# Expert rounds of a two-layer kernel: the next pair's first product ahead of the convolution, and ScalarE's weight copies behind it

## What is computed

```
xn = layernorm(x)
u, v = xn @ Wu + bu, xn @ Wv + bv
y = (u * causal_fft_conv(v, h)) @ Wo + bo
per token: top-2 of 8 experts by softmax(xn @ Wg)
   expert e: relu(xn @ W1[e] + b1[e]) @ W2[e] + b2[e]   (128 -> 256 -> 128)
x = x + y + sum over the two experts of probability * expert output
```

## Time and profile before

| | us |
|---|---|
| median of three runs | 493.45 (492.63 to 493.6) |
| the profiled execution, its own time | 493.04 |
| its span, first to last instruction | 491.2 |
| PE matmul busy | 366.0 (75%), weight loads 298.7 (61%) |
| DVE busy | 294.4 (60%) |
| ACT busy | 225.9 (46%) |
| POOL busy | 258.4 (53%) |

### The profile page before, as it was taken

The page is one execution under the profiler, slowest core; times in us unless marked ns, Lnnn a source line. Parts: engine busy times, 40 slices in busy tenths (PEclk is TensorE's granted clock), DMA queues, the critical chain, the costliest instruction groups (busy, mean ns, idle before and its releaser), DMA issues.

```text
span 491.2 us, 7805 instructions
## 1 busy us (share of the span) xinstructions
PE 366.0 (75%) x2302; PEld 298.7 (61%) x2302; DVE 294.4 (60%) x782; ACT 225.9 (46%) x551; POOL 258.4 (53%) x254
## 2 busy tenths in 40 slices
PE   2485588869997975949997978898887777766720
PEld 0272255658675644737996867787776667755620
DVE  3977569614773796474688993478438772244105
ACT  1373042325332316334343066434567676687724
POOL 2754766733666323016566676666666555365540
PEclk9999599997998999687998999999999999999975
DMA  9999999823321330001111282445322215422407
GB/s 211 396 197 262 166 140 135 268 51 85 87 75 40 111 89 1 1 5 39 34 34 37 69 261 75 142 140 151 112 69 75 63 29 158 137 74 74 126 11 252
DMA packets 64744, 55.05 MB, mean 112 GB/s; under 512 B 6819, under 2 KB 56683, under 8 KB 64446
## 3 DMA queue, kind: packets, MB, share of 16 engines
q1 hardware_dynamic: 57888, 41.71, 35.6%
q0 software_dynamic: 6656, 12.51, 8.4%
q10 hardware_dynamic: 158, 0.33, 0.4%
HBM read 30.44 MB, written 25.27 MB: 113 GB/s over the span
## 4 chain that ended last, share of the span: by engine, by line
PE 44%; issue 13%; ACT 12%; DVE 10%; DMA 10%; POOL 8%; SPq 1%; ACTq 0%; POOLq 0%; DVEq 0%
PE psS L1161 19%; PE psO L1161 15%; PE psT L1161 7%; ACT hT L1122 7%; POOL slots L826 4%; DMA slots<-row,slot 4%; DMA moe<-ys,xs 2%; POOL w L847 2%; DMA xres<-in_x 2%; ACT row L1027 1%; PE psT L1263 1%; POOL moe L836 1%; DVE work L1713 1%; DVE xres L1747 1%; DMA moe<-ys,ring 1%
## 5 line engine op out<-in xcount | busy, mean ns | idle before, releaser
L813 POOL DMA_INDIRECT slots<-row,slot x64 | 69.3, 1083 | 57.0 <-DVE slot L1580 22.4
L836 POOL DMA_INDIRECT moe<-ys,xs x61 | 61.1, 1001 | 58.3 <-issue 16.6
L1161 PE MATMUL psO<-ring,hT 128*128 128x128 f32 x320 | 45.2, 284 | 45.1 <-ACT hT L1122 45.1
L1161 PEld LDWEIGHTS psO<-ring,hT 128*128 128x128 f32 x320 | 38.7, 191 | 53.4 <-issue 53.4
L1122 ACT ACTIVATE hT<-psT,ring 128x128 f32<-128x128 f32 x160 | 45.6, 368 | 45.7 <-PE psT L1161 45.7
L1868 DVE TENSOR_TENSOR ys<-psO,ring 128x256 f32<-128x256 f32 x40 | 17.0, 424 | 75.3 <-PE psO L1161 75.1
L1055 ACT ACTIVATE ring<-w 128x642 f32 x80 | 55.9, 761 | 1.1 <-issue 1.0
L1161 PE MATMUL psS<-work 128*128 128x512 f32 (+3 forms) x96 | 42.6, 558 | 12.6 <-DVE work L1696 8.8
L836 POOL DMA_INDIRECT moe<-ys,w x35 | 38.0, 1087 | 23.3 <-DVE ys L1868 9.7
L1020 ACT ACTIVATE work<-psT 128x512 f32<-128x512 f32 (+3 forms) x32 | 16.5, 516 | 66.6 <-PE psT L1263 66.6
L826 POOL DMA_INDIRECT slots<-row,slot x32 | 34.9, 1091 | 18.1 <-DMA slots<-row,slot 10.9
(11 more groups left out here) (272 smaller groups left out, 781.4 us busy)
## 6 DMA issues: line engine op xcount, KB each, us to landing
slots<-xs SPq DMA_DIRECT2D x14, 516.0 KB, 14.7
mats<-in_iv SPq DMA_DIRECT2D x16, 256.0 KB, 3.7
xs<-slots SPq DMA_DIRECT2D x61, 64.5 KB, 1.9
w<-in_w SPq DMA_DIRECT2D x8, 321.0 KB
w<-slots SPq DMA_DIRECT2D x35, 64.5 KB, 1.9
xres<-in_x SPq DMA_DIRECT2D x4, 512.0 KB, 9.7
mats<-in_fw SPq DMA_DIRECT2D x1, 2048.0 KB, 11.3
moe<-xs SPq DMA_DIRECT2D x4, 512.0 KB, 7.8
```

What stands on the lines that cost most here:

```text
L813: pool.indirect_dma_start(slots1[:, :], bass.IndirectOffsetOnAxis(ap=(slot1, slot2)[k][:, i:i + 1], axis=0), row[:, i, :], None, bounds_ch ...
L836: pool.indirect_dma_start(dst[:, :], bass.IndirectOffsetOnAxis(ap=row_slots[l][m][:, D:ROWW].bitcast(I32), axis=0), ys[:, n % UNROLL, :], ...
L1161: return pe.matmul(o, lhsT, rhs, start=start, stop=stop)
```

## The change

On TensorE `expert_hidden(r + 1)` moves up, directly behind `expert_out(r)` and ahead of the convolution. On ScalarE `hidden(r + 1)` moves to the front of the round, and `copy_weights(r + 2)` from the front to behind the convolution's copies, directly ahead of `take_rows(r + 2)`. No instruction is added or removed; VectorE, GpSimd and SyncE keep their order.

```diff
             for r in range(PRELUDE, PAIRS1):
-                if 0 <= r + 2 < PAIRS1:
-                    copy_weights(r + 2)
+                if 0 <= r + 1 < PAIRS1:
+                    hidden(r + 1)
                 for kind, k in conv_at(r):
...
                     if kind == "yt":
                         take_y(k)
-                if 0 <= r + 1 < PAIRS1:
-                    hidden(r + 1)
                 if 0 <= r + 2 < PAIRS1:
+                    copy_weights(r + 2)
                     take_rows(r + 2)
...
             for r in range(PRELUDE, PAIRS1):
                 if 0 <= r:
                     expert_out(r)
+                if 0 <= r + 1 < PAIRS1:
+                    expert_hidden(r + 1)
                 for kind, k in conv_at(r):
...
                     if kind == "wo":
                         project_y(k)
-                if 0 <= r + 1 < PAIRS1:
-                    expert_hidden(r + 1)
                 if 0 <= r + 2 < PAIRS1:
                     expert_rows(r + 2)
```

## The result

| | before | after |
|---|---|---|
| median, us | 493.04 (491.58 to 493.6, 4 runs) | 497.99 (496.73 to 499.92, 4 runs) |
| profiled execution, its own time | 493.04 | 496.73 |
| its span | 491.2 | 494.8 |
| from the first relu to the last | 186.1 | 189.3 |

The ratio after to before is 1.0108 (95% interval 1.0062 to 1.0155): slower, by 3 to 8 us. A second set of nine executions gave 1.0081 (1.0051 to 1.0111). The forecast was 496.9 against the 493.45 known then, a ratio of 1.0070. Ratios leave out an execution that took over 1.5% more than the fastest of its kernel; that was one only, of `copies_ahead`.

What follows compares the result with a forecast made beforehand. The prediction took the expert loop (second product, convolution, first product, relu) as the bound. Terms +9.8 + 4.6 - 5.4 - 4.4 + 1.2 - 1.5 - 0.7 - 0.1 = +3.5 us gave 496.9, range 494.2 to 499.3.

Steps and rivals of the forecast that it cites:

- The copies in the loop: ScalarE's weight copies and row copy enter the loop from relu to relu; the next first product waits for both.
- Plain turns: Relu-to-relu turns without convolution, `yt` or `wo` work: 3.92 us against 3.345, 17 turns, +9.8 us.
- `wo` turns: Two rounds with no bank for ScalarE to copy: 3.92 us against 4.69, -1.5 us.
- `yt` and `yt` + `wo` turns: Turns with a `yt` bank copy: 4.38 us; six `yt` + `wo` from 5.12, -4.4; two `yt` from 3.78, +1.2.
- Forward turns: Four turns where copies lie beside the convolution and TensorE sets the pace: 5.46 us, -1.34 each, -5.4 us.
- Neither GpSimd nor VectorE held them up: Rival in forward rounds: GpSimd's four issues take 6.05 us, or VectorE's waits bind; 2.4 us more, 499.3; chance 0.14.
- the ring: Eight output tiles, four rounds deep, let GpSimd lag in forward rounds; rounds 8 and 9 give the time back.
- Inverse turns: Eight turns with copies behind the convolution's second bank copy, register reads uncovered: 7.37 us against 6.80, +4.6 us.
- Reads by the page: Inverse turns: covered reads would give 6.82 us; a read floor of some 600 ns would add some 0.3 each.
- A slow read: One of 80 register reads took 952 ns, median 278; named on top of the inverse turns' upper bound.
- Start: Relu 0 no longer sits behind the copies of pair 1: 283.15 instead of 283.88, -0.7 us.
- the 17 turns of the rival: Rival: TensorE's clock falls to 1.2 GHz, lengthening 17 plain turns by some 15 us, to 512; chance 0.03.

Runs made afterwards that it cites:

- copies_ahead: Against the changed kernel, ScalarE copies the weights of pair r + 3 instead of r + 2, behind the row copy; 475.24 us, ratio 0.9698 to the kernel before.
- act_alone: Against the kernel before, only ScalarE's new order, TensorE as before; median 506.18 us, ratio 1.0297.
- the better half alone: Against the kernel before, only TensorE's new order, ScalarE as before; median 485.83 us, ratio 0.9863.
- mats_early: Against the changed kernel, SyncE issues the second half's inverse matrices two row loads earlier; median 496.54 us, ratio 1.0084 to the kernel before.
- copies_first: Against the changed kernel, ScalarE's weight copies stand directly behind the relu, ahead of the bank copies; median 491.09 us, ratio 0.9973 to the kernel before.

## Why the prediction was right

- **The copies in the loop**: right, and the main cost. Plain turns 3.92 (forecast 3.92), `wo` turns 3.92 (3.92), `yt` and `yt` + `wo` turns 4.40 (4.38). `act_alone` shows it by itself.
- **Forward turns**: 5.46 (5.46), four of them, in every profiled execution of the changed kernel. Neither GpSimd nor VectorE held them up; the lag was taken by the ring, as argued. But the price showed elsewhere: the matrix of class 1 for the second half's inverse landed 5.2 and 9.2 us ahead of its product in the two profiles before, and 2.8, 0.3 and 3.7 ahead in the three after.
- **Inverse turns**: 7.05 instead of 7.37. The mechanism was right (reads uncovered behind a waited bank copy), the size was not: I took 2.26 us from the second take to the row copy, from a row ahead of the rounds; it measured 1.98 (0.69 and 1.29). The reads took 0.28 us here, 0.48 and 0.41 there. Eight turns (6.99 to 7.16), 2.5 us too much. The signs were off with it: the first product waited 1.32 us for the row copy, not 1.6, and the gap ahead of the copies is 0.09 (306.02 + 0.60 to 306.71), not 0.2 to 0.3. In plain turns that wait is 0.30, as forecast.
- **Reads by the page**: that the sequencer reads on while an instruction waits (the Trainium skill, Advanced Engine Details and Errata, section Sequencer Loop) does not show for the register reads here: the read starts 0.06 us behind the start of the bank copy that waited (306.02, 306.08), not ahead of it. What holds it back, no run takes apart. The floor of 600 ns (the Trainium skill, DMA: Bandwidth & Descriptors, section Latency and other measured facts) is not seen either: the median is 277 ns.
- **A slow read**: I named the 952 ns read only for the upper bound of the inverse turns. It is one turn in each of the three profiles, +1.3 us, and it stands in a plain turn that I had at 3.92 with all reads covered. This term was missing.
- **Start**: the first relu came 1.63 us behind the row copy of pair 0, as worked out (before 2.36): -0.7. **Tail**: -0.2 (-0.1).
- **Clock**: single turns at 1.2 GHz in some executions of several kernels, the one before included, never the 17 turns of the rival, and none in the rounds of the changed kernel's three profiles; single turns had no place in my sum.

The rounds were forecast at 190.4 us and took 189.3: 2.5 less in the inverse turns, 1.3 more for slow reads, 0.2 in the `yt` turns. These errors offset each other in part, and what is left makes the sum 1.2 too high: it says +3.5, the profiles account for +2.3 (3.2 in the rounds, -0.7, -0.2). The medians differ by 4.4 to 5.0. The other 2.1 to 2.7 us are in no term of the sum, and that the time comes out 1.1 above the forecast and not below it is theirs: that the total was met so closely is in part luck. Single turns at the lower clock and the stretch ahead of the rounds can carry them, but how often they strike in either kernel was not counted, so that part stays open.

## What to carry to other kernels

Moving a wait off the critical engine is half of the work: ask what stands between that wait and the next one on the other engine, and count each small copy there, once for every round, the rounds without the big work included. A register read that hides behind queued work costs nothing; right behind a waited instruction it costs all its latency, and during heavy transfers over three times that. Of a change with two halves, price each alone: here the better half alone, and the copies one pair further ahead, both beat the kernel before.

## What was not expected of the hardware

- Register reads of 0.28 us took 0.89 to 0.99 us while DMA was at its full share (273 to 290 GB/s in those stretches), in every kernel that had them there, the one before included.
- TensorE fell to 1.2 GHz after a turn with idles of 1.61 and 1.11 us (`mats_early`), and after 1.64 and 1.10 (`copies_first`), while in three executions of the changed kernel turn 34 had the same idles and the clock stayed. It also fell in the first round of the kernel before (8.44 us for that turn) in one of two executions.
